# Routing by token number in a six-stage decoder kernel: scatters carry numbers, tiles gather rows, and the last group's routing is placed by hand

## The reference

```python
x = x + attn0(_layernorm(x))            # 16 heads of 128, causal
x = x + wkv(_layernorm(x), ctx)         # recurrence over the 128 tokens of a sequence
x = x + moe(_layernorm(x))              # 16 experts of 176, 4 chosen per token, and a shared one of 704
x = x + attn1(_layernorm(x))            # 16 heads of 16
x = x + xattn(_layernorm(x), ctx)       # cross-attention, 16 heads of 128
x = x + bit_ffn(_layernorm(x))          # ternary weights
```

```python
logits = h @ router_w.T
probs = jax.nn.softmax(logits)
top_vals, top_idx = jax.lax.top_k(probs, K)                 # K = 4 of E = 16
top_vals = top_vals / jnp.maximum(top_vals.sum(-1, keepdims=True), 1e-09)
routed = sum over the 4 chosen e of  top_val[e] * (silu(h @ w_gate[e]) * (h @ w_up[e])) @ w_down[e]
shared = silu(h @ sh_gate) * (h @ sh_up) @ sh_down
out = routed + sigmoid(h @ sh_gate_w) * shared
```

## Time and profile before

| | us |
|---|---|
| median of 3 runs | 1974.43 |
| lowest and highest run | 1970.72 and 1980.58 |
| the profiled execution | 1987.48 |
| its span in the trace | 1985.7 |
| busy: PE, DVE | 1656.2, 1233.1 |
| busy: ACT, POOL | 870.7, 545.3 |

### The profile page before, as it was taken

The page is one execution under the profiler, slowest core; times in us unless marked ns, Lnnn a source line. Parts: engine busy times, 40 slices in busy tenths (PEclk is TensorE's granted clock), DMA queues, the critical chain, the costliest instruction groups (busy, mean ns, idle before and its releaser), DMA issues. The chain is left out here.

```text
span 1985.7 us, 25633 instructions
## 1 busy us (share of the span) xinstructions
PE 1656.2 (83%) x8566; PEld 1319.4 (66%) x8566; DVE 1233.1 (62%) x2690; ACT 870.7 (44%) x2514; POOL 545.3 (27%) x442
## 2 busy tenths in 40 slices
PE   6977788987988744779999668789887999999866
PEld 5866677876877633557777446667665888788644
DVE  4643367577657736425443556766665778877878
ACT  4533334443443322312223134456434666666756
POOL 2222232362253051230001455545113122311000
PEclk9988889998999876989999757989889999999989
DMA  7255442231121024223332311100101110000001
GB/s 272 103 190 181 156 168 96 87 110 48 59 91 54 22 101 117 66 67 106 104 108 88 115 33 33 32 11 1 43 1 40 28 48 27 31 1 1 1 1 43
DMA packets 81414, 143.23 MB, mean 72 GB/s; under 512 B 8452, under 2 KB 43780, under 8 KB 81156
## 3 DMA queue, kind: packets, MB, share of 16 engines
q1 hardware_dynamic: 75140, 124.81, 19.2%
q0 software_dynamic: 6144, 16.79, 2.6%
HBM read 86.90 MB, written 54.66 MB: 71 GB/s over the span
## 5 line engine op out<-in xcount | busy, mean ns | idle before, releaser
L552 PE MATMUL bank<-x_channel_major,qkv_weights_split 128*128 128x512 f32 x256 | 120.1, 469 | 48.3 <-POOL qkv_weights_split L2403 43.3
L2082 ACT ACTIVATE self_attention<-self_attention,small 128x128 f32<-128x128 f32 x256 | 100.0, 392 | 116.4 <-DVE small L1446 115.5
L703 PE MATMUL bank<-self_attention 128*128 128x256 f32 x512 | 134.6, 410 | 17.0 <-DVE residual L1465 14.0
L2586 POOL TENSOR_TENSOR cross_attention_heads<-cross_attention_heads 128x512 f32<-128x512 f32 x64 | 70.4, 1100 | 285.3 <-DVE cross_attention_heads L1798 285.2
L2298 ACT ACTIVATE cross_attention_heads<-cross_attention_heads,small 128x128 f32<-128x128 f32 x256 | 99.6, 390 | 90.3 <-DVE small L1822 90.3
L2214 ACT ACTIVATE narrow_attention<-bank,small 128x128 f32<-128x128 f32 x256 | 90.4, 365 | 108.2 <-DVE small L1688 103.5
L1048 PE MATMUL bank<-cross_attention,cross_attention_heads 128*128 128x256 f32 x512 | 124.4, 386 | 15.0 <-DVE residual L1836 10.2
L703 PEld LDWEIGHTS bank<-self_attention 128*128 128x128 f32 x512 | 104.9, 209 | 38.2 <-DVE residual L1465 17.7
L2451 POOL DMA_INDIRECT narrow_attention<-picked_outputs,dispatch x64 | 62.6, 977 | 242.0 <-DMA picked_outputs<-tiles 208.4
L2401 POOL CAST qkv_weights_split<-self_attention 128x1024 fp32r<-128x1024 f32 x45 | 48.9, 1087 | 289.6 <-DMA self_attention<-in_wqkv 252.7
L1048 PEld LDWEIGHTS bank<-cross_attention,cross_attention_heads 128*128 128x128 f32 x512 | 95.2, 190 | 38.2 <-DVE residual L1836 22.4
(11 more groups left out here) (363 smaller groups left out, 4689.7 us busy)
## 6 DMA issues: line engine op xcount, KB each, us to landing
picked_inputs<-self_attention SPq DMA_DIRECT2D x32, 1024.0 KB, 10.4
self_attention<-in_wqkv SPq DMA_DIRECT2D x48, 512.0 KB
experts_far<-picked_inputs SPq DMA_DIRECT2D x79, 128.0 KB, 2.1
picked_outputs<-tiles SPq DMA_DIRECT2D x79, 128.0 KB, 1.7
self_attention<-in_wo SPq DMA_DIRECT2D x16, 512.0 KB, 4.0
experts<-in_moe SPq DMA_DIRECT2D x4, 1408.0 KB, 12.6
self_attention<-in_bv SPq DMA_DIRECT2D x16, 256.0 KB, 4.1
bitnet_weights<-in_bitgu SPq DMA_DIRECT2D x8, 416.0 KB, 3.4
```

The source lines that it names most:

```text
L552: T.matmul(out_ap, w_hi, x_hi, start=first, stop=False)
L703: m = T.matmul(bank[7][:, 0:D], ZT_a[n % 2][:, h, :], wo_a[p % 2][:, h, :], start=h == 0, stop=h == HG - 1)
L2082: m = S.activation(P_a[u][:, h, :], P_a[u][:, h, :], ACT.Exp, bias=negmax_a[u][:, h:h + 1], accum_out=sums_a[u][:, h:h + 1])
L2586: G.tensor_tensor(x_qsq, x_queries[f % 2], x_queries[f % 2], ALU.mult).then_inc(x_squared, 1)
```

## The change

- `picked_inputs` and its zero fills go. A DRAM tensor `expert_inputs` holds the normalised rows by token (`keep`: one 512 KB write per group, from SyncE), and `picked_by` holds a token number (4 bytes) per row; it is zeroed by one small transfer.
- The 64 scatters write token numbers (4 bytes each) to `picked_by` instead of 1 KB rows.
- For every tile SyncE fetches 128 token numbers (`fetch_tokens`, 79 transfers of 512 bytes), all of them ahead of the first `store_tile`; GpSimd then fetches the tile's 128 rows by an indirect DMA (`fetch_tile`), four tiles ahead.
- The order of the groups in the shared units is 0, 1, 2, 3: group 3's six units come after the tiles, so the loop no longer waits for its placing. The loop makes two side steps per unit. Group 3's side work is one generator per engine (`last_group`), whose steps are placed one against the other. GpSimd makes the products of group 3 too. From unit 15 on (`DVE_UNIT`) VectorE subtracts in the split of the result.
- Weight slices 0 and 1 are split in the last iterations of the self-attention (VectorE and GpSimd); slices 2 to 5 by ScalarE and GpSimd in the loop, three units ahead. The value fetches of group 3 move ahead of the wait for the end of the self-attention.

```diff
-ZERO_ROWS = 1024
+DVE_UNIT = 15
-SHARED = [0, 1, 3, 2]
+SHARED = [0, 1, 2, 3]
...
# loop of the units, TensorE (the other engines alike)
-            side.add(wkv_group(NG - 1), routing(NG - 1), dispatch(NG - 1), make_tables())
+            side.finish()
+            side.add(last_group())
             for i in range(NBEFORE + LAG):
                 if i < NBEFORE:
-                    while UNITS[i][0] == NG - 1 and NG - 1 not in done:
-                        side.step()
                     up(i)
-                side.step(3)
+                side.step()
                 if i >= LAG:
                     down(i - LAG)
-                side.step(3)
+                side.step()
...
# VectorE, in the loop
+                    if i >= DVE_UNIT:
+                        split_hidden(i)
# VectorE and GpSimd, in the self-attention's loop
+                if n in (NSTEP, NSTEP + 1):
+                    split_weights(n - NSTEP)
...
# GpSimd
             def scatter(g, b):
-                    G.indirect_dma_start(picked_x, bass.IndirectOffsetOnAxis(slots[:, c:c + 1], 0), tiles_xn[i % 2][:, b, :],
+                    G.indirect_dma_start(picked_by, bass.IndirectOffsetOnAxis(slots[:, c:c + 1], 0), tokens[:, bb:bb + 1],
                                          None).then_inc(scattered, 16)
+            def last_group():
+                yield from pause(6)
+                wkv_helps(KT * (NG - 1))
+                yield from pause(7)
+                wkv_helps(KT * (NG - 1) + 1)
+                yield from pause(17)
+                for b in range(GB):
+                    scatter(NG - 1, b)
+                yield
+            def fetch_tile(n):
+                pool.wait_ge(*tokens_of(n))
+                pool.wait_ge(t_turned, n - NXS + 1)
+                G.indirect_dma_start(t_in[n % NXS], None, rows_x,
+                                     bass.IndirectOffsetOnAxis(tile_tokens[:, n:n + 1], 0)).then_inc(got_in[n % NXS], 16)
...
+            split_weights(2)
             for i in range(NBEFORE + LAG):
-                if i + 2 < NSH:
-                    split_weights(i + 2)
+                if i + 3 < NSH:
+                    split_weights(i + 3)
+                if i < DVE_UNIT:
                     up(i)
-                side.step(6)
+                side.step(2)
             side.finish()
+            pool.wait_ge(kept_x, 16 * NG)
+            for n in range(NTILE):
+                fetch_tile(n)
             for bb in range(GB + 2):
                 gather(bb)
...
# SyncE
-                for i in range(5 * (p - 1), min(5 * p, E * NT // ZERO_ROWS + 2)):
-                    zero(i)
+                if p >= 2 * NHG and p % NHG == 0:
+                    keep(p // NHG - 2)
...
-            def fetch_tile(n):
+            def fetch_tokens(n):
                 if n % 4 == 0:
                     nc.sync.load(rows[n:n + 4], row_at[:, n:n + 4])
-                sp.wait_ge(t_turned, n - NXS + 1)
-                D_(t_in[n % NXS], picked_x[row(n), :]).then_inc(got_in[n % NXS], 16)
+                D_(tile_tokens[:, n:n + 1], picked_by[row(n), :]).then_inc(tokens_of(n)[0].sem, 16)
...
+            keep(NG - 1)
             sp.wait_ge(tables_set, 1)
             sp.wait_ge(scattered, 16 * B * TOPK)
-            for n in range(NXS):
-                fetch_tile(n)
-            for s in range(NTILE + 3):
-                if s + NXS < NTILE:
-                    fetch_tile(s + NXS)
-                if s >= 3:
-                    store_tile(s - 3)
+            for n in range(NTILE):
+                fetch_tokens(n)
+            for n in range(NTILE):
+                store_tile(n)
```

456 lines of the change are left out of this document (328 added, 128 removed).

## The result

The kernel with the change takes 2007.15 us (median of 4 runs, 2004.15 to 2010.71) against 1974.51 us (median of 4, 1970.72 to 1980.58). The ratio is 1.0163, with an interval of 1.0131 to 1.0195: slower by some 32 us, where 1896 was predicted. The profiled execution took 2010.71 us.

What follows compares the result with a forecast made beforehand. It took TensorE as busy nearly everywhere except self-attention steps with zero fills and the shared expert's units. 46 us from the fills and 32 from units and tiles' start made 78: 1974.4 - 78 = 1896, range 1865 to 1932.

Steps and rivals of the forecast that it cites:

- rival (d): Tiles' start: token fetches pay their landings one after the other, 2.1 us each, stall 145 us, time 2021; chance 0.05.
- S: End of the shared units: time when all scatters have landed, predicted at 820 us, bounds 806 and 857.
- The zero fills: Self-attention: removing the fills from seven steps saves 46 us, bounds 29 to 56.
- the row of 133.4: Self-attention step with fills, standing for three without recurrence: 44.5 to 45.0 us each, to become 33.
- The scatters' way back: Scatters of 4-byte pieces: taken to cost GpSimd 0.96 us and 0.3 between two, as with 1 KB rows.
- The units: Shared expert after the self-attention: a new pace brings all token numbers into DRAM at 820 us.
- TensorE's start of unit 2: Shared units: waits for GpSimd's split of slice 2, behind group 2's scatters, until 719 us.
- Units 2 to 7: Shared units: VectorE sets the pace, 6.4 us each, 38 in all, plus 3 for adding group 0 up.
- units 8 to 14 with the routing: Shared units: 4.2 us plus 0.8 for waits each, 38 in all, picks placed at about 798 us.
- Rival (b): Shared units keep their old pace of 8.9 us, S becomes 857, time 1932; chance 0.14.
- The last scatters: After the picks are placed: the scatters take 20.0 us and land 1.9 us later.
- The start of the tiles: Tile 0 in at 827 us, a 20 us stall behind the token fetches; 33 us gained, 32 taken.

Runs made afterwards that it cites:

- pitch64: The changed kernel with 4-byte token numbers scattered 64 bytes apart instead of side by side; 1950.13 us, one run.
- piece64: The changed kernel with token numbers scattered in 64-byte pieces, 64 bytes apart; 1944.96 us, one run.
- loop: The change's new order of units, routing and splits, with the kernel before's 1 KB rows, zero fills and tile fetches; 1955.91 us, ratio 0.9861.
- late_scatters: ahead8 with group 2's 16 scatters issued two at a time beside units 7 to 14; 1929.26 us, ratio 0.9694.
- ahead8: wide_ahead with 8 tiles' token numbers fetched before the first store instead of 24; 1915.39 us, ratio 0.9700.
- quarter_wkv: loop with VectorE's part of the last group's recurrence cut to one of four sequences (output differs); 1944.54 us, one run.
- ahead: The changed kernel with 24 tiles' token numbers fetched first, then one fetch per store; 1986.13 us, ratio 1.0055.
- wide_ahead: piece64 and ahead together; 1937.24 us, ratio 0.9768.
- the probe: Separate program with only groups of 16 scatters and SyncE's direct lines at several distances; a group took 34.1 us at 4 bytes, 21.2 at 64.

## Why the prediction was wrong, point by point

**The step that failed** is this one: "The scatters keep their count. No row shows one with pieces of 4 bytes; the nearest is 0.96 us on GpSimd and 0.3 between two, for 128 rows of 1 KB ... I take the same". The issue does cost the same, 0.96 and 0.3. The landing does not: the sum took 1.9 us for it, as for a gather, and 20.9 were measured. It put nothing at all for what slow landings do to the weights' fetches, and there 39 us went. No row of before could show the landing of pieces side by side, and I bounded the unknown by the issue on GpSimd alone. The only adverse end that I named for 4-byte pieces stood in rival (d), and there for the fetches, not for the scatters. The price follows from the runs. From pitch64 and piece64 to the changed kernel it is 0.029 to 0.031 of the time, 57 to 62 us. By the profiled executions of piece64 and of the changed kernel it is 66: 38 in the attention (its end at 663 or 701), and some 28 up to S (144 or 173 us after that end), of which 19 are the last group's late landing and some 9 the late slices (below).

**The zero fills.** Predicted 46 us off, bounds 29 to 56. The output weights of step 9 come 41.8 us earlier (351.9 instead of 393.7), and without the slow scatters the attention ends 39 us earlier. Mechanism right, size 4 to 7 too high. Two of the three steps without a recurrence run at 32.6 and 32.5 us, as predicted (33). The third, from 88.1, takes 37.4; the prediction let the row of 133.4 stand for it, and these 4 us are the difference. The wait of the earlier trace rows is gone.

**The scatters' way back.** I listed who stands behind a scatter on GpSimd, but not who stands behind it in the DMA engines. The thirds of the weights do. This is where 39 us of the 42 went. The Trainium skill ("DMA: Bandwidth & Descriptors", Back-pressure in remote DMA) states, for transfers between cores, that stalled writes stall the source engine's other queues too. The share of 0.88 at 23 GB/s agrees, here with writes to DRAM. The Trainium skill ("DMA: Bandwidth & Descriptors", Specifications) also says that below 512 bytes the DMA engine reads, modifies and writes. Size alone does not explain these runs: scatters of 4-byte pieces at 16 or 64 bytes land in 2.2 us, rows of 1 KB in 2.6. As the reason why neighbours are slow it is plausible, and no run shows it.

**The units.** Predicted: S 118 us after the attention's end. Measured with fast scatters: 144. It splits as follows. TensorE's start of unit 2: 719 predicted, 718.6 in loop, but not for the reason given. I had it wait for GpSimd's split behind group 2's scatters. The rows name the normalised tiles instead, and late_scatters confirms them, so the hit on 719 was luck. VectorE makes these tiles behind the products of units 0 and 1, and these wait for ScalarE, which in ahead8 stands 13.3 us until slice 2's weights land at 670.2. In the changed kernel that landing is late as well (17 us after the attention's end instead of 4, beside group 2's scatters), and TensorE's wait grows to:

```profile
...
728.24 1.35 PE L579 MATMUL bank<-identity,normalised_tiles 128*128 128x128 f32 x4 [21.87 <-DVE normalised_tiles L1241]
...
```

Units 2 to 7: 41 us predicted, 45 measured. The 41 has an error in it: two chunks over six units are three units a chunk, not 3.5, which would have given 46. That this is near is luck too, since quarter_wkv shows that VectorE's work is mostly not what paces these units. The term that was mis-sized is units 8 to 14 with the routing: 38 predicted, 58 measured. I took 4.2 us per unit plus 0.8 for waits, from rows of before in which the routing was over. In loop units 8 to 13 take 7.8 us each with no engine full, and the waits go round: GpSimd waits 37.5 us for ScalarE there, ScalarE 24 for TensorE, VectorE 8 for TensorE and 7 for ScalarE. That this chain of waits sets the pace is read from the waits; no run tested it for these units. Rival (b), 8.9 us a unit, was nearer than the forecast: S at 857 against 820 predicted and 845 in loop.

**The last scatters.** Predicted 20.0 us and 1.9 to land. With 64-byte pieces it is exactly that (S comes 1.9 us after the last issue in piece64), with 4 bytes side by side 20.9.

**The start of the tiles.** Predicted: tile 0 in at S + 6.7, first store at S + 41, a stall of 20. Measured in the changed kernel: TensorE's first tile row at S + 7.3, the first store at S + 48.2. The fetches with their register loads cost 0.61 us each, not 0.52. By the prediction's own formula that makes the stall 27 instead of 20, and the runs agree: from S to the last store the changed kernel takes 234.7 us, piece64 233.7 and ahead8, without the stall, 207.1. ahead gets back only 21 or 22 of the 27, because in it, as in wide_ahead, tile 4 waits for the 20 fetches that share its semaphore; in the changed kernel this wait is hidden behind the stall. Mechanism right, size 7 too low. Rival (d) did not happen: issues overlap with landings. The tiles run at 2.49 us from store to store, as before.

**The sum** with fast scatters: -78 predicted; 4 to 7 us less from the fills, 26 less from the units and 7 less from the start of the tiles make it some -40. piece64's ratio says -30, in one run, and its profiled execution is 42 under that of the kernel before, which the prediction puts 13 us above the median of its runs. So the terms account for most of the miss, with up to 10 us left open, and the scatters' landing accounts for the change of sign.

## What to carry to other kernels

When a transfer shrinks, ask where its pieces land and who shares the place, not only how many bytes and issues it has. A table of 4-byte entries that is scattered entry by entry should be spread out (16 bytes were enough here), at the price of some 0.5 MB of zeros. And whoever stands behind the transfer in the DMA engines belongs in the sum like whoever stands behind it on the issuing engine. Issue small fetches that a loop needs as the loop goes, a few ahead, with a semaphore value for each, not all before the first store.

## What the runs showed of the hardware that was not expected

- 16 indirect scatters of 128 pieces of 4 bytes have landed 1.3 us after the last issue when the pieces are 16 bytes or more apart, 8.7 at 8 bytes and 13 to 14 at 4 bytes. The size of a piece (4 bytes, 1 KB) hardly matters: 1.3 and 1.7 us.
- It is the same for direct transfers from SyncE: a line of 128 pieces of 4 bytes lands in 5.0 to 6.5 us when they are packed and in 1.4 to 1.8 when they are 64 bytes apart. SyncE's issue does not show it.
- While packed scatters are under way, transfers of other queues are held: in slices of 10 us the DMA engines show 0.81 to 0.97 busy at 23 to 48 GB/s, and a step with three fetches of 512 KB takes 65.8 us instead of 40.0.
- The small packets of the probe's scatters hardly count as busy time of the DMA engines (0.01 to 0.02, with 4-byte pieces at any distance). The cost shows only in landings and in what other packets take.
- A zero fill does not cost by its bytes: 1 MB hides in a step of 32.9 us, 5.2 MB in pieces of 2 KB cost 12 us (44.8 against 32.6), and 4.2 MB in pieces of 1 KB cost 19 (51.3 against 32.6). Per piece the two are alike: 2560 and 4096 pieces make 4.8 and 4.6 ns each, an estimate from these steps.
